# First attention: the products for the row maxima from the high halves alone, in alternating halves of the array

## What is computed

```python
scores = jnp.einsum('bnhd,bmhd->bhnm', Q, K)          # 16 heads, head width 64, 2048 x 2048
scores = scores * (SCALE * adaptive_scale)[None, :, None, None] / TEMP
w = jax.nn.softmax(scores, axis=-1)
attn = jnp.einsum('bhnm,bmhd->bnhd', w, V).reshape(B, N, H * HD)
```

## Time and profile before

| what | before |
|---|---|
| median of 3 runs | 1927.22 us (1925.53 to 1928.65) |
| span of the profiled execution | 1927.3 us |
| PE busy | 96 %, PEld 65 % |
| POOL busy | 83 % |
| ACT busy | 80 % |
| DVE busy | 75 % |
| first attention, first to last step | about 52 to 1203 us of the span |

### The profile page before, as it was taken

How to read it: one execution, slowest core, us unless ns; L and a number is a source line. 1 busy time by engine, 2 the same in 40 slices (tenths; PEclk the granted TensorE clock), 3 DMA queues, 4 the chain that set the end, 5 groups by cost and what they waited for, 6 DMA issues and landing times.

```text
span 1927.3 us, 55726 instructions
## 1 busy us (share of the span) xinstructions
PE 1854.3 (96%) x23471; PEld 1256.4 (65%) x23471; DVE 1443.6 (75%) x2647; ACT 1548.5 (80%) x1921; POOL 1597.5 (83%) x1025
## 2 busy tenths in 40 slices
PE   4899999999999999999999998779999999999998
PEld 3566666666666666666666665547777777767766
DVE  7798878878878878878878875566767767767652
ACT  4799999999999999999999999646666666666664
POOL 3899999999999999999999999358688787787752
PEclk8999999999999999999999999889999999999999
DMA  6101100100100100100100100100000000000000
GB/s 148 35 11 26 34 15 22 35 17 20 35 19 18 35 19 18 35 19 17 35 23 14 35 2 2 55 1 2 2 1 2 2 2 2 2 1 1 2 2 23
DMA packets 45034, 37.96 MB, mean 20 GB/s; under 512 B 8304, under 2 KB 44144, under 8 KB 44528
## 3 DMA queue, kind: packets, MB, share of 16 engines
q1 hardware_dynamic: 44304, 34.00, 7.0%
q10 hardware_dynamic: 480, 0.39, 0.1%
HBM read 8.15 MB, written 1.05 MB: 5 GB/s over the span
## 4 chain that ended last, share of the span: by engine, by line
PE 87%; DVE 4%; POOL 3%; issue 3%; ACT 2%; DMA 0%; SPq 0%; POOLq 0%; DVEq 0%; ACTq 0%
PE ST L1639 11%; PE ST L1640 11%; PE RING L1520 7%; PE OO L1601 6%; PE OO L1603 6%; PE OO L1600 6%; PE OO L1520 4%; PE ST L1832 3%; PE ST L1838 3%; PE ST L1837 3%; PE ST L1839 3%; POOL PBUF L704 2%; PE OO L1859 2%; PE OO L1861 2%; PE OO L1863 2%
## 5 line engine op out<-in xcount | busy, mean ns | idle before, releaser
L620 POOL TENSOR_TENSOR PAB<-PR,PAB 128x1024 f16<-128x1024 f32 x342 | 724.3, 2134 | 42.3 <-ACT PAB L799 42.2
L799 ACT ACTIVATE PAB<-ST,exp_scale 128x1024 f16<-128x1024 f32 x512 | 567.6, 1109 | 0.0
L1104 DVE TENSOR_REDUCE maxes<-RING 128x1 f32<-128x512 f32 x661 | 439.6, 684 | 122.6 <-PE RING L1520 118.2
L1600 PE MATMUL OO<-VP,PAB 128*128 128x66 f16 x4096 | 446.6, 192 | 2.9 <-POOL PAB L620 2.9
L1601 PE MATMUL OO<-VP,PAB 128*128 128x64 f16 x4096 | 447.1, 193 | 0.0
L1603 PE MATMUL OO<-VP,PAB 128*128 128x66 f16 x4096 | 445.1, 192 | 0.0
L797 ACT ACTIVATE PR<-ST,exp_scale 128x1024 f32<-128x1024 f32 x342 | 381.9, 1117 | 64.7 <-PE ST L1640 61.8
L1600 PEld LDWEIGHTS OO<-VP,PAB 128*128 128x128 f16 x4096 | 380.2, 96 | 78.3 <-issue 15.5
L1601 PEld LDWEIGHTS OO<-VP,PAB 128*128 128x128 f16 x4096 | 377.0, 97 | 60.6
L1639 PE MATMUL ST<-QL,KH 128*128 128x512 f16 x1024 | 388.6, 380 | 2.0 <-DVE QH L1116 1.0
L1640 PE MATMUL ST<-QH,KL 128*128 128x512 f16 x1024 | 388.8, 380 | 0.0
(11 more groups left out here) (319 smaller groups left out, 4027.8 us busy)
## 6 DMA issues: line engine op xcount, KB each, us to landing
KH<-HS SPq DMA_DIRECT2D x124, 64.0 KB, 2.0
QL<-HS SPq DMA_DIRECT2D x64, 64.0 KB, 2.0
QL<-LS SPq DMA_DIRECT2D x64, 64.0 KB, 2.0
QH<-HS SPq DMA_DIRECT2D x64, 64.0 KB, 2.0
KL<-LS SPq DMA_DIRECT2D x62, 64.0 KB, 2.0
X<-in_L_attn_a_x SPq DMA_DIRECT2D x4, 256.0 KB, 4.2
SHARED<-in_rope_cos SPq DMA_DIRECT2D x1, 1024.0 KB, 5.2
SHARED<-in_rope_sin SPq DMA_DIRECT2D x1, 1024.0 KB, 7.3
```

The source lines that it names most:

```text
L620: pool.tensor_tensor(PB[:, s, :], PRA[g % PR_SLOTS], PA[:, s, :], ALU.subtract).then_inc(p_low_ready, 1)
L799: act.activation(PA[:, step % SLOTS_A, :], ST[step % 2][:, :], ACT.Exp, scale=scale).then_inc(sa.exps, 1)
L1104: dve.reduce_max(maxes[:, i // BLOCKS, i % BLOCKS:i % BLOCKS + 1], bank[:, :], X_AXIS).then_inc(sa.ring_taken, 1)
L1600: pe.matmul(o, high, v[:, 0:V2_AT], start=(m == 0 and qt == 0), stop=False, skip_group_check=True)
```

## The change

The maxima products use the high part of the queries only, and read 64 rows instead of 128. For an even key block the queries' high part comes from rows 0 to 63 of `QL16` and the keys from rows 0 to 63 of `KH16`; for an odd key block both come from rows 64 to 127, the queries from `QH16`. The stationary and the moving operand then lie in one half of the array's rows. Number, order, width (128x512 out), banks, waits and signals of the products stay as they are. The low part of the queries no longer enters the maximum; the shift is then a slightly different number, which is the same for numerator and denominator of the softmax.

```diff
@@ max_a
                 qt, c = divmod(i, BLOCKS)
                 at = qb * BLK + qt * P
-                pe.matmul(RING3[item % 3][:, :], QL16[head % 2][:, at:at + P], KH16[head % 2][:, c * BLK:(c + 1) * BLK],
+                queries, rows_of = ((QL16, slice(0, DA)), (QH16, slice(DA, P)))[c % 2]
+                pe.matmul(RING3[item % 3][:, :], queries[head % 2][rows_of, at:at + P],
+                          KH16[head % 2][rows_of, c * BLK:(c + 1) * BLK],
                           start=True, stop=True).then_inc(sa.ring_put, 1)
```

## The result

The changed kernel takes 1931.42 us (median of 18 runs, 1929.34 to 1932.25), the kernel before in the same comparison 1927.54 us (18 runs): a ratio of 1.0017, with a 95 % interval from 1.0010 to 1.0024. That is within the 0.2 % that I called no change, on its slower side. I had forecast 1867 us. The number lies inside the wide range that I gave, but that is luck: the forecast and its direction were wrong, and the range reached so far up only for the slower rival, whose price was wrong as well.

The account below looks back on a forecast made before the run. TensorE was taken to bound the first attention at 2.224 us a step; 0.186 us saved a pair lets GpSimd take over at 2.09 to 2.10: 1927.3 - 62 + 2 = 1867 us, range 1860 to 1885.

Parts of the forecast that it names:

- wide range: Whole kernel time from 1860 to 2010 us, leaving out 0.17 above and 0.03 below.
- slower rival: The switch drains the array: a pair costs 0.142 to 0.342 us more, 1998 to 2098 us; chance 0.34.
- What bounds the kernel: First attention: TensorE bounds the steps at 2.224 us each, GpSimd stands next at 2.09 to 2.10 us.
- Part 1: Maxima products: reading 64 rows instead of 128 costs nothing in either direction.
- Part 2: The two maxima products of a step overlap, the second costing 0.03 us instead of 0.216: 0.186 us saved a pair.
- Part 3: Changing between 128 and 64 rows twice a step costs zero; upper bound 0.164 plus 0.10 us at each switch.
- no change: Within 0.2 %, some 4 us; rival: halves take turns, second product 0.216 us after the first, 1927 us; chance 0.11.
- Part 5: Waits around the maxima: VectorE has the bank free, TensorE's wait there stays at 2.8 us in 1100.
- The sign that I named: Distances from last scores product to maxima and from maxima to value product: 0.216 us without drain, 0.38 or more with.

Follow-up runs that it names:

- e1: The changed kernel with all maxima products in rows 0 to 63, so that no two can run side by side: 2034.28 us, ratio 1.0552.
- e2: The changed kernel with each pair of maxima products issued twice in a row over the same banks: 2033.74 us, ratio 1.0552.
- e4: The kernel before without 7 of the 8 value products with the low part in each step: 1860.78 us, ratio 0.9658.
- e3: The changed kernel with the maxima pair between the two halves of the value products, except in step 3 of a unit: 1953.16 us, ratio 1.0134.
- e5: The changed kernel with the maxima products of step 2 of each unit reading all 128 rows again: 1930.06 us against 1930.61 for the change.

## Why the prediction was wrong

**What bounds the kernel: right.** TensorE bounds the steps, shown by e1 and e2, where 0.205 and 0.209 us more a step (means of steps 64 to 447) cost 103 us, all of it. GpSimd stands next at 2.09 us, shown by e4: 1860.8 us against the 1865 that my working gives for such a saving.

**Part 1, fewer rows cost nothing by themselves: right, as far as the runs tell.** The 0.226 us instead of 0.216 in e1 are no price of the rows, as the way out is shorter by as much; they belong to the switch.

**Part 2, two products side by side: right, and I had it too dear.** They start 0.003 us apart, where I took 0.03. The saving is 0.2125 us a pair. The Trainium skill's 4 ns ("TensorE: Matmul & The Clock Gate", Part 3) agrees with this trace.

**Part 3, the change of shape at no cost: the step that failed.** I put it at nothing. It costs 0.096 us going in and 0.103 going out, and 0.010 more behind the first value product: 0.209 a pair against 0.2125 won. What the engine does is wait with the first load of weights in the new shape. That load comes 0.307 to 0.315 us after a product of 512 columns started, over steps 64 to 447 and outside step 3, where full products load theirs 0.001 to 0.002 us after such a start. The rule of the Trainium skill that changing the tiling mode drains the engine ("TensorEngine Tiling (Array Packing)", Key Properties) agrees with this for the rows. I argued it away with two rows. The earlier trace rows has a product with fewer columns, which is indeed free; it says nothing on rows, and the trace doesn't tell whether that product changes the mode at all. The earlier trace rows has 16 columns and a slow load of weights: its 0.18 us leave room for just such a wait, as I noted myself, and I took zero rather than the middle. With 0.1 us at each switch from that room the sum would have been 0.186 won and 0.2 lost, some 7 us slower over the 500 pairs, close to what came. My slower rival was the right mechanism at the wrong price: it waited for the recorded end of a product (0.164 us) and an uncovered load (0.10), and the runs show 0.096 and 0.103 in place of both. My 0.11 for no change stood on halves that take turns, which they don't; that a switch could take just what the overlap gives, I had no rival for.

**Part 5, the waits stay as they are: wrong in one place.** I asked whether VectorE would have the bank free, and it has. I didn't ask what is queued behind the maxima on VectorE. It is the normalisation, for which the first value product of each unit waits; before, it came with 0.08 us to spare. The trace had a sign of it that I left out of the earlier trace rows: 60 late loads at L1600, about one a unit, 15.3 us together. The switch delays the maxima of step 2 by 0.1 us, and step 3 grew by 0.055 us in each of 64 units, 3.5 us. With some 3 ns won in the other steps the kernel is 1.8 us slower over steps 64 to 510. The rest of the measured 3.3 to 3.9 us I don't assign: the other stretches vary by as much between kernels that do the same there.

**The sign that I named** (0.216 without a drain, 0.38 or more with one) was too coarse: it was 0.31.

## What to carry to other kernels

Products over 64 rows in opposite halves of the array do run together, but each change between 64 and 128 rows costs about 0.1 us of a TensorE that is the bound. One pair of 512 columns between two changes breaks even; by e2 a gain would come only with more products in a group, for which there must be banks. A zero for an unseen cost needs a row of the same kind (rows for rows, not columns for rows); where the nearest row leaves room for a wait, a value inside that room is the estimate, not its lower end. And when a product is made later, look at what the engine that takes its result does next, not only at whether it is free.

## What the runs showed of the hardware

- A change from 128 to 64 rows costs 0.095 us behind a product of 66 columns (e3) and 0.096 behind one of 512; back to 128 rows it costs 0.092 (e1, e2). What follows the first product behind a change comes about 0.010 us later as well, in either direction; so the way out is 0.103 in the change, where the first pair is also the last. The transposes over 4 columns between full products are followed after 0.11 us and hold nobody up.
- Two products in opposite halves start 0.003 us apart; a second pair starts 0.226 us after the first (e2), and so does a second product in the same half (e1).
- The list of waits puts the time of a switch down to the semaphore that came last ("DVE maxes"), or to "issue". Such a wait, regular and on the first load of a new shape, isn't one for that engine: step 2 of e5 claims the same banks and has none, and in e1 the same 0.312 us stand under "issue".
